# Softmax sums in four 32-column tiles, their inverses spread over partitions by DMA

## The chip, the cores and the metric

The kernel runs on one core of a Trainium2 chip. Its time is the device time of one execution in microseconds (us); before the change it is 820.48 us, the median of three runs (820.0 to 821.76). Five engines work side by side, each through its own instructions in order: TensorE (PE; its weight loads are shown as PEld), VectorE (DVE), ScalarE (ACT), GpSimd (POOL) and SyncE (SP), which here only issues DMAs. They wait for each other by semaphores.

## The reference, cut to what matters

Two transformer layers with different attention and feed-forward parts. The change lies in the attention of layer 0 alone: batch 2, sequence 1024, width 128, 16 query heads over 4 key/value groups, 64 columns a head.

```python
xn = _layernorm(x, ln_scale, ln_bias)
q = (xn @ Wq) per head; k, v = split(xn @ Wkv) per group
q, k = _layernorm(q, ...), _layernorm(k, ...)
dots = jnp.einsum('bghqd,bgkd->bghqk', qg, k) * scale
attn = jax.nn.softmax(dots, axis=-1)
out = jnp.einsum('bghqk,bgkd->bghqd', attn, v)
return out @ Wout
```

The softmax needs, for each head and query, the sum over 1024 keys of the exponentials and its inverse; the kernel multiplies by that inverse after the product with v.

## The kernel before, in words

**Slots.** The attention of a batch is done in 16 slots, one for 256 queries and one group of four heads. The four heads of a slot stand as two halves of the partitions (h = 0, 1: 64 partitions each) and two pairs side by side in the columns (hp = 0, 1: 256 columns each). So a slot's unscaled output is 128 partitions x 512 columns.

**What a slot does.** (1) Scores with queries on the partitions, in eight units (`unit_scores`, L689); VectorE takes each row's maximum (`largest`, L1276, L1278, L1280, L1290), ScalarE copies half of most units aside for it (L992). SP puts the maxima into a spare row of the queries by eight small DMAs (L416), so that (2) the scores with keys on the partitions (`tile_scores`, L709) come out with the maximum taken off. (3) ScalarE's exponentials (`exps`, L973). (4) GpSimd adds the eight tiles of exponentials up: five additions in a row (L544), and one (L549) of a pair that VectorE adds first (`add_tail`, L1298). (5) TensorE's product with v (`tile_values`, L724), in two column tiles of 64. (6) The sums over keys (`add_up`, L739): a matrix of ones of 64 columns times GpSimd's total, in two column tiles, which gives on each of a half's 64 partitions the sum of every (pair, query) column. (7) ScalarE makes a first inverse as exp(-ln(sum)) into `rinv` (`take_log` L999, `invert` L1004), VectorE improves it by one Newton step in PSUM (`correct`, L1363 and L1366). (8) ScalarE copies the output from PSUM into `ot` (`keep_out`, L980), VectorE multiplies it there by the inverse (`scale`, L1372), (9) TensorE projects it (`project_out`, L752) and VectorE adds it to x (`add`, L1381).

**Order.** It is written out by hand. `attention` of each engine runs over phases, four to a slot. With slot m's units in phases 4m to 4m+3, its exponentials' tiles run five phases behind and the product six behind; `add_up` stands at the end of phase 4m+10 on TensorE, the inverse in 4m+11 on ScalarE. VectorE corrects at the end of 4m+11 and in the middle of 4m+12 (steps 0 and 1) and scales at the end of 4m+12, behind the second maximum of that phase and ahead of those of 4m+13; in 4m+13 it adds the tail of slot m+1. TensorE projects at the end of 4m+13. Units exist up to phase 63, so scale is followed by maxima in slots 0 to 12.

TensorE may compute a new unit only when VectorE has reduced the one before (the score banks are single): `unit_scores` waits for `part_made`. SP's queue holds, for every slot in turn, the eight DMAs of its maxima, each pair behind its wait, then after both batches the loads of the two chosen experts' weights of layer 0's feed-forward part. Slot 15 of each batch is finished in the code that follows its loop. In the last phases of batch 1 VectorE also sums the rows of the first batch, chooses the experts (L1348) and makes the low parts of their weights (L1443), ScalarE the high parts (L1061); TensorE's first product with them is L1832.

Of the kernel before, what the change touches and what calls it, by code (L numbers as in the profile page):

```python
# [166 lines left out]
def up_weights(wproj):  # L167

    return wproj[:, 0:TOP * HID].rearrange("p (k f) -> p k f", f=HID)
# [7 lines left out]
def first_layer(nc, a, xv, x, ident, wt, psum, sb, sem, c):  # L177

    with ExitStack() as own:
        def mine(name, shape, dt=F32):  # L180
            return sb(name, shape, dt, own)
# [8 lines left out]
        vecs = mine("vecs", [P, 4, DH])  # L190
        cross = mine("cross", [P, 4, DH])
# [21 lines left out]
        acc = [work[:, 2 * i * UW:(2 * i + 1) * UW].rearrange("p (h q) -> p h q", h=2) for i in range(2)]  # L213
        tail = work[:, UW:2 * UW].rearrange("p (h q) -> p h q", h=2)
        ot = work[:, 3 * UW:3 * UW + WIDE]
        rinv = work[:, 3 * UW + WIDE:4 * UW]

        def spare(k):
            return space[:, (4 + k) * UW:(5 + k) * UW]

        pt = [spare(k).rearrange("p (h q) -> p h q", h=2) for k in range(TILES)]
# [8 lines left out]
        raw = wt[:, :]  # L230
        rawi = wt[:, W_GATE * P:].bitcast(I32)
        diagonal = rinv[:, 0:P]
        aside_at = [xnt[:, 0, i * 512:(i + 1) * 512] for i in range(2)]

        x_in = [sem(f"x_in{b}") for b in range(BATCH)]
# [60 lines left out]
        pool_added = sem("pool_added")  # L296
        pv_made = sem("pv_made")
        out_kept = sem("out_kept")
        sums_made = sem("sums_made")
        log_made = sem("log_made")  # L300
        rinv_made = sem("rinv_made")
        fix_made = sem("fix_made")
        ot_made = sem("ot_made")
        y_made = sem("y_made")
# [38 lines left out]
        def banks(first, n):  # L343
            return psum[:, first * 512:(first + n) * 512]
# [16 lines left out]
        sums = banks(7, 1)  # L361
        LAST = BATCH * SLOTS - 1

        def sums_of(n):

            return banks(5, 1) if n == LAST else sums

        def rows(h):
            return slice(h * DH, (h + 1) * DH)

        def place(m):
            return divmod(m, GROUPS)

# [12 lines left out]
        def queries(t, m):  # L386
            at, g = place(m)
            return t[:, PAIRS * g:PAIRS * (g + 1), at * QB:(at + 1) * QB]

        def sync_part(sp):  # L390
            for h in range(2):
                sp.dma_start(x[:, 0, h * T:(h + 1) * T], xv[0][:, h * T:(h + 1) * T]).then_inc(x_in[0], 16)
            sp.dma_start(wproj[:, K_AT:K_AT + KV], a["L0_attn_Wkv"][:, 0:KV]).then_inc(wkv_in, 16)
            sp.dma_start(wproj[:, V_AT:V_AT + KV], a["L0_attn_Wkv"][:, KV:2 * KV]).then_inc(wkv_in, 16)
            sp.dma_start(wproj[:, Q_AT:Q_AT + INNER], a["L0_attn_Wq"]).then_inc(wq_in, 16)
            sp.dma_start(x[:, 1], xv[1]).then_inc(x_in[1], 16)
            sp.dma_start(raw[:, 0:2 * P].rearrange("p (t d) -> p t d", t=2), a["L1_attn_Wu"].rearrange("(t p) d -> p t d", p=P)).then_inc(r_in, 16)
            sp.dma_start(raw[:, 2 * P:4 * P].rearrange("p (t d) -> p t d", t=2), a["L1_attn_Wv"].rearrange("(t p) d -> p t d", p=P)).then_inc(r_in, 16)
            sp.dma_start(raw[:, 4 * P:5 * P], a["L1_attn_Wb"]).then_inc(r_in, 16)
            sp.dma_start(raw[:, W_O * P:W_GATE * P], a["L1_attn_Wo"]).then_inc(r_in, 16)  # L400
            sp.dma_start(rawi[:, 0:HID1].rearrange("p (t d) -> p t d", t=HT), a["L1_ffn_w_gate"].rearrange("(t p) d -> p t d", p=P)).then_inc(r_in, 16)
            sp.dma_start(rawi[:, HID1:2 * HID1].rearrange("p (t d) -> p t d", t=HT), a["L1_ffn_w_up"].rearrange("(t p) d -> p t d", p=P)).then_inc(r_in, 16)
            sp.dma_start(rawi[:, 2 * HID1:3 * HID1], a["L1_ffn_w_down"]).then_inc(r_in, 16)
            sp.dma_start(wout[:, :, :], a["L0_attn_Wout"].rearrange("(h p) d -> p h d", p=P)).then_inc(wout_in, 16)
            for dst, src in small:
                sp.dma_start(dst, src).then_inc(shared_in, 16)
            for b in range(BATCH):
                for m in range(SLOTS):
                    n = SLOTS * b + m
                    at, g = place(m)  # L410
                    sp.wait_ge(ql_made, TILES * b + 2 * at + 2)
                    for pair in range(4):
                        t, hp = divmod(pair, PAIRS)
                        sp.wait_ge(max_made, 4 * n + pair + 1)
                        for h in range(2):
                            sp.dma_start(ql[h * DH:h * DH + 1, PAIRS * g + hp, at * QB + t * P:at * QB + (t + 1) * P].bitcast(F32),  # L416
                                         nmx[n % 2][:, pair, h:h + 1], allow_slow_non_contiguous=True).then_inc(max_placed[n % 2], 16)
            sp.wait_ge(chosen0_made, 1)
            es = [sp.value_load(chosen[0:1, 0, k:k + 1], min_val=0, max_val=EXPERTS - 1) for k in range(TOP)]
            for k, e in enumerate(es):  # L420
                sp.dma_start(up_weights(wproj)[:, k, :], a["L0_ffn_W1"][bass.ds(e, 1), :, :].rearrange("e d f -> d (e f)")).then_inc(c["up_in"][0], 16)
            for k, e in enumerate(es):
                sp.dma_start(c["b1s"][:, 0, k, :], a["L0_ffn_b1"][bass.ds(e, 1), :].rearrange("e (t f) -> f (e t)", f=P), allow_slow_non_contiguous=True).then_inc(c["b1_in"][0], 16)
            for k, e in enumerate(es):
                sp.dma_start(down_weights(wproj)[:, k, :, :], a["L0_ffn_W2"][bass.ds(e, 1), :, :].rearrange("e (t f) d -> f (e t) d", f=P)).then_inc(c["down_in"][0], 16)
                sp.dma_start(c["b2s"][:, 0, k, :], a["L0_ffn_b2"][bass.ds(e, 1), :]).then_inc(c["down_in"][0], 16)
# [130 lines left out]
        def tensor_part(pe):  # L557
# [170 lines left out]
            def add_up(n):  # L728

                if n and n < LAST:  # L730
                    pe.wait_ge(x_added, n)
                terms = [acc[n % 2]]
                if n % SLOTS == SLOTS - 1:
                    terms = [pt[TILES - 2], pt[TILES - 1], acc[n % 2]]
                for k, term in enumerate(terms):
                    if k == len(terms) - 1:
                        pe.wait_ge(pool_added, ADDS * (n + 1))
                    for h in range(2):
                        last = pe.matmul(sums_of(n)[rows(h), :], c["ones_square"][:, 0:DH], term[:, h, :],  # L739
                                         start=(k == 0), stop=(k == len(terms) - 1))  # L740
                last.then_inc(sums_made, 1)
# [145 lines left out]
        def scalar_part(act):  # L887
# [106 lines left out]
            def take_log(n):  # L994

                act.wait_ge(sums_made, n + 1)
                if n:
                    act.wait_ge(ot_made, n)
                act.activation(rinv, sums_of(n), ACT.Ln).then_inc(log_made, 1)  # L999

            def invert(n):

                act.wait_ge(log_made, n + 1)
                act.activation(rinv, rinv, ACT.Exp, scale=-1.0).then_inc(rinv_made, 1)  # L1004

            def produce(b):

# [144 lines left out]
        def vector_part(dve):  # L1152
# [198 lines left out]
            def weights_of_chosen():  # L1351
# [4 lines left out]
                route_link(dve.reciprocal(wv[:, 0, 0:1], r[:, 6, 1:2]))  # L1356
                dve.tensor_tensor(wv[:, 0, 1:2], wv[:, 0, 0:1], r[:, 6, 0:1], ALU.mult).then_inc(wv0_made, 1)

            def correct(n, step):

                if step == 0:
                    dve.wait_ge(rinv_made, n + 1)
                    dve.tensor_tensor(sums_of(n), sums_of(n), rinv, ALU.mult).then_inc(fix_made, 1)  # L1363
                else:
                    dve.wait_ge(fix_made, 2 * n + 1)
                    dve.scalar_tensor_tensor(out=sums_of(n), in0=sums_of(n), scalar=2.0, in1=rinv, op0=ALU.subtract, op1=ALU.mult).then_inc(fix_made, 1)  # L1366

            def scale(n):

                dve.wait_ge(fix_made, 2 * n + 2)  # L1370
                dve.wait_ge(out_kept, n + 1)
                dve.tensor_tensor(ot, ot, sums_of(n), ALU.mult).then_inc(ot_made, 1)  # L1372

            def add(n):

# [25 lines left out]
            def attention(b, end):  # L1401

                for ph in range(LAG + 1, end):
                    mine_at, mine_k = divmod(ph, 4)
                    m, k = divmod(ph - LAG - 5, 4)
                    n = SLOTS * b + m
                    if mine_at < SLOTS:
                        largest(SLOTS * b + mine_at, 2 * mine_k)
                    if k == 0 and 0 < m <= SLOTS:
                        add(n - 1)  # L1410
                    if k == 2 and 0 <= m < SLOTS:
                        correct(n, 1)
                    if mine_at < SLOTS:
                        largest(SLOTS * b + mine_at, 2 * mine_k + 1)
                    if k == 1 and 0 <= m < SLOTS:
                        correct(n, 0)
                    if k == 2 and 0 <= m < SLOTS:
                        scale(n)
# [953 lines left out]
```

## Time and profile before

| | |
|---|---|
| median of three runs | 820.48 us |
| profiled execution | 819.98 us, span 818.2 |
| instructions | 14237 |
| HBM traffic | 5.92 MB read, 1.05 MB written |
| DMA | 49745 packets, 8.03 MB |

The rows of the trace are given as times in microseconds from the span's start. In a timeline or a chain the first number is the start, the second the length; "x8" counts instructions that are merged into one row, and the bracket says how long the engine was idle before and who ended it. Only compute counts as busy; matmul ends are modelled.

### The profile page before, as it was taken

Reading aid. Unit: us, or ns where it says so; the run is one execution under the profiler, and the core shown is the slowest. Engines: PE = TensorE matmul, PEld = TensorE weight load, DVE = VectorE, ACT = ScalarE, POOL = GpSimd, SP = SyncE. Lnnn points to the kernel's source line nnn. Section 1 sums busy time; section 2 is a strip of 40 time slices with the busy share of each in tenths; the row PEclk is TensorE's granted clock in tenths of the full one; section 3 lists DMA queues with packets and bytes.
Section 4 is the critical chain, followed back from the end, with each engine's and each line's share of the span. In section 5 each row is a group of like instructions: output and inputs, shape, how many; then the busy total and the mean of one; then the engine's idle time right before and its main releaser. Section 6 shows DMA issues by size and latency. Waiting matters only on the chain.

```text
span 818.2 us, 14237 instructions
## 1 busy us (share of the span) xinstructions
PE 790.9 (97%) x5002; PEld 474.4 (58%) x5002; DVE 631.3 (77%) x1147; ACT 524.8 (64%) x955; POOL 589.1 (72%) x385
## 2 busy tenths in 40 slices
PE   6998999999999999999899999999999999999998
PEld 5664455455555555566544555555555555987787
DVE  6997788888888787376867788887888877678774
ACT  3865576676667776668655766666777666555522
POOL 2777587888888888946558888788988796455840
PEclk9999999999999999999999999999999999999999
DMA  6000000000000000000000000000000002200001
GB/s 183 1 2 1 0 2 2 1 1 1 1 1 2 1 2 1 1 1 1 1 1 2 1 1 1 2 1 2 1 1 1 2 1 53 56 1 2 1 1 52
DMA packets 49745, 8.03 MB, mean 10 GB/s; under 512 B 42502, under 2 KB 48266, under 8 KB 49674
## 3 DMA queue, kind: packets, MB, share of 16 engines
q1 hardware_dynamic: 48810, 6.99, 5.4%
q8 instruction: 40, 0.66, 0.4%
q14 instruction: 31, 0.25, 0.1%
q10 hardware_dynamic: 864, 0.13, 0.1%
HBM read 5.92 MB, written 1.05 MB: 9 GB/s over the span
## 4 chain that ended last, share of the span: by engine, by line
PE 88%; DVE 6%; ACT 2%; issue 2%; POOL 1%; DMA 1%; SPq 0%; DVEq 0%; POOLq 0%; ACTq 0%
PE psum L724 29%; PE psum L709 21%; PE psum L689 10%; PE psum L739 4%; PE psum L1846 4%; PE psum L752 3%; DVE part L1280 2%; PE psum L1857 2%; PE psum L575 2%; PE psum L1884 2%; PE psum L577 1%; PE psum L576 1%; PE psum L1914 1%; PE psum L1832 1%; PE psum L668 1%
## 5 line engine op out<-in xcount | busy, mean ns | idle before, releaser
L544 POOL TENSOR_TENSOR space<-space 128x1024 f32<-128x1024 f32 x160 | 381.6, 2385 | 23.7 <-ACT space L973 5.7
L973 ACT ACTIVATE space<-psum 128x512 f32<-128x512 f32 x512 | 264.2, 606 | 37.2 <-PE psum L709 36.3
L724 PE MATMUL psum<-space,vb 128*64 128x512 f32 x1024 | 247.5, 605 | 2.1 <-ACT space L973 2.1
L1280 DVE TENSOR_REDUCE part<-psum 128x2 f32<-128x1024 f32 x150 | 183.0, 1220 | 32.0 <-PE psum L689 32.0
L724 PEld LDWEIGHTS psum<-space,vb 128*64 128x64 f32 x1024 | 62.5, 136 | 120.3 <-issue 60.8
L549 POOL TENSOR_TENSOR space<-space 128x1024 f32<-128x1024 f32 x30 | 71.7, 2389 | 79.8 <-DVE space L1298 79.8
L689 PE MATMUL psum<-kh,qh 64*128 64x512 f32 x512 | 119.0, 453 | 4.5 <-DVE part L1280 4.5
L1276 DVE TENSOR_REDUCE part<-psum 128x1 f32<-128x512 f32 x106 | 73.2, 690 | 53.4 <-PE psum L689 53.4
L709 PE MATMUL psum<-qh,kh 64*128 64x512 f32 x512 | 105.8, 395 | 0.0
L709 PE MATMUL psum<-qh,kl 64*128 64x512 f32 x512 | 105.2, 389 | 0.0
L689 PEld LDWEIGHTS psum<-kh,qh 64*128 64x128 f32 x512 | 49.9, 183 | 95.4 <-DVE part L1280 57.4
L709 PE MATMUL psum<-ql,kh 64*128 64x512 f32 x512 | 104.9, 390 | 0.0
L992 ACT ACTIVATE xnt<-psum 128x512 f32<-128x512 f32 x106 | 63.1, 595 | 47.7 <-PE psum L689 47.7
L1278 DVE TENSOR_REDUCE part<-xnt 128x1 f32<-128x512 f32 x106 | 72.6, 685 | 1.9 <-ACT xnt L992 0.3
L709 PEld LDWEIGHTS psum<-qh,kl 64*128 64x128 f32 x512 | 51.9, 184 | 7.7
L709 PEld LDWEIGHTS psum<-qh,kh 64*128 64x128 f32 x512 | 50.5, 185 | 10.0 <-ACT space L973 3.2
L709 PEld LDWEIGHTS psum<-ql,kh 64*128 64x128 f32 x512 | 51.6, 184 | 8.0
L999 ACT ACTIVATE space<-psum 128x512 f32<-128x512 f32 x32 | 19.2, 600 | 52.0 <-PE psum L739 52.0
L1298 DVE TENSOR_TENSOR space<-space 128x512 f32<-128x512 f32 x60 | 46.0, 807 | 2.7 <-ACT space L973 2.7
L980 ACT ACTIVATE space<-psum 128x512 f32<-128x512 f32 x32 | 19.2, 599 | 43.0 <-PE psum L752 41.7
L1747 POOL TENSOR_TENSOR inv<-inv,half_power 128x4 f32<-128x4 f32 x18 | 18.7, 1043 | 38.0 <-DVE inv L2095 26.3
L752 PEld LDWEIGHTS psum<-wout,space 128*64 128x64 f32 x512 | 30.0, 137 | 17.8 <-issue 17.1
(252 smaller groups left out, 1134.5 us busy)
## 6 DMA issues: line engine op xcount, KB each, us to landing
ql<-nmx SPq DMA_DIRECT2D x256, 0.5 KB, 2.0
wproj<-in_L_ffn_W SPq DMA_DIRECT2D x4, 256.0 KB, 3.5
out<-x SPq DMA_DIRECT2D x3, 256.0 KB, 2.0
x<-in_L_attn_x SPq DMA_DIRECT2D x2, 256.0 KB, 4.4
wproj<-in_L_attn_Wq SPq DMA_DIRECT2D x1, 512.0 KB, 6.6
x<-in_L_attn_x SPq DMA_DIRECT2D x1, 512.0 KB, 7.5
wout<-in_L_attn_Wout SPq DMA_DIRECT2D x1, 512.0 KB, 7.1
w1s<-in_L_ffn_W SPq DMA_DIRECT2D x2, 256.0 KB, 2.8
```

Source lines behind the costliest of these rows:

```text
L544: pool.tensor_tensor(to, pt[0] if u == 1 else to, pt[u], ALU.add)\
L549: pool.tensor_tensor(to, to, tail, ALU.add).then_inc(pool_added, 1)
L689: last = pe.matmul(scores[:, h * 512:(h + 1) * 512], qh[rows(h), PAIRS * g + hp, at * QB + t * P:at * QB + (t + 1) * P], kh[rows(h), g, ha ...
L709: last = pe.matmul(key_scores[kt % 2][h].rearrange("p (a q) -> p a q", a=PAIRS), key[rows(h), g, keys], queries(query[rows(h)], m), start= ...
L724: last = pe.matmul(outp[rows(h), :], vb[:, place(m)[1], kt, :], pt[kt][:, h, :], start=(kt == 0), stop=(kt == TILES - 1))
L752: last = pe.matmul(sums_of(n)[rows(s), t * P:(t + 1) * P], ot[:, at:at + DH], wout[:, PAIRS * g + hp, :], start=(hp == 0), stop=(hp == PAI ...
L973: act.activation(pt[kt][:, h, :], key_scores[kt % 2][h], ACT.Exp).then_inc(exp_made, 1)
L992: act.activation(aside_at[i % 2], scores[:, 512:1024], ACT.Copy).then_inc(unit_kept, 1)
L1276: dve.tensor_reduce(to[:, 0, 0:1], scores[:, 0:512], AX_X, ALU.max, negate=True).then_inc(part_made, 1)
L1278: dve.tensor_reduce(to[:, 0, 1:2], aside_at[i % 2], AX_X, ALU.max, negate=True).then_inc(kept_read, 1)
L1280: dve.tensor_reduce(to[:, half, :], scores.rearrange("p (h k) -> p h k", h=2), AX_X, ALU.max, negate=True)\
L1298: dve.tensor_tensor(tail[:, h, :], pt[TILES - 2][:, h, :], pt[TILES - 1][:, h, :], ALU.add).then_inc(tail_made, 1)
```

## The change

All slots but the last of each batch (`is_brief`) form their sums in another way. The matrix of ones has 32 columns, and the four (half, pair) combinations of a slot go to four column tiles of 32 partitions, each over 256 columns. So `sums` holds 128 partitions x 256 columns, the four heads one below another. Ln, Exp and the Newton step work on that shape, in two small tiles that are free by then (`guess_at`, `brief`); both correction steps stand together in phase 4m+11. The result lies in SBUF with a head on 32 partitions, where `ot` has a head on 64 partitions of one pair's columns; so SP copies each head's 32 rows twice into `rinv` (eight DMAs of 32 x 1 KB a slot, `spread_rinv`), behind the maxima of the slot two later, and for the last of these slots ahead of what SP does next. `scale` waits for these copies and multiplies `ot` by `rinv`, both in SBUF.

```diff
+        def spread_rinv(sp, n):
+            sp.wait_ge(fix_made, 2 * n + 2)
+            for h in range(2):
+                for hp in range(PAIRS):
+                    for first in (h * DH, h * DH + DH // 2):
+                        sp.dma_start(rinv[first:first + DH // 2, hp * QB:(hp + 1) * QB], brief[brief_rows(h, hp), :]).then_inc(rinv_spread, 16)
...
                             sp.dma_start(ql[...], nmx[n % 2][:, pair, h:h + 1], ...).then_inc(max_placed[n % 2], 16)
+                    if m >= 2:
+                        spread_rinv(sp, n - 2)
+                spread_rinv(sp, SLOTS * b + SLOTS - 2)
             sp.wait_ge(chosen0_made, 1)
...
+                if is_brief(n):
+                    pe.wait_ge(pool_added, ADDS * (n + 1))
+                    for h in range(2):
+                        for hp in range(PAIRS):
+                            last = pe.matmul(sums[brief_rows(h, hp), 0:QB], c["ones_square"][:, 0:P // 4], acc[n % 2][:, h, hp * QB:(hp + 1) * QB],
+                                             start=True, stop=True)
+                    last.then_inc(sums_made, 1)
+                    return
...
+            def correct_brief(n):
+                at = sums[:, 0:QB]
+                dve.wait_ge(rinv_made, n + 1)
+                dve.tensor_tensor(at, at, guess_at, ALU.mult).then_inc(fix_made, 1)
+                dve.wait_ge(fix_made, 2 * n + 1)
+                dve.scalar_tensor_tensor(out=brief, in0=at, scalar=2.0, in1=guess_at, op0=ALU.subtract, op1=ALU.mult).then_inc(fix_made, 1)
...
             def scale(n):
-                dve.wait_ge(fix_made, 2 * n + 2)
                 dve.wait_ge(out_kept, n + 1)
-                dve.tensor_tensor(ot, ot, sums_of(n), ALU.mult).then_inc(ot_made, 1)
+                if is_brief(n):
+                    dve.wait_ge(rinv_spread, spread_count(n))
+                    dve.tensor_tensor(ot, ot, rinv, ALU.mult).then_inc(ot_made, 1)
+                else:
+                    dve.wait_ge(fix_made, 2 * n + 2)
+                    dve.tensor_tensor(ot, ot, sums_of(n), ALU.mult).then_inc(ot_made, 1)
...
-                    if k == 2 and 0 <= m < SLOTS:
+                    if k == 2 and m == SLOTS - 1:
                         correct(n, 1)
...
-                    if k == 1 and 0 <= m < SLOTS:
+                    if k == 1 and 0 <= m < SLOTS - 1:
+                        correct_brief(n)
+                    if k == 1 and m == SLOTS - 1:
                         correct(n, 0)
```

## Rows read from the trace of the kernel before

**Rows 1.** The page: busy time by engine; the chain that ended last, by engine.

```profile
PE 790.9 (97%) x5002; PEld 474.4 (58%) x5002; DVE 631.3 (77%) x1147; ACT 524.8 (64%) x955; POOL 589.1 (72%) x385
...
PE 88%; DVE 6%; ACT 2%; issue 2%; POOL 1%; DMA 1%; SPq 0%; DVEq 0%; POOLq 0%; ACTq 0%
```

**Rows 2.** Busy time in one slot: PE, PEld, DVE, ACT, POOL; clock, DMA.

```profile
193.00:210.46 17.46, 17.46 (x122) 9.33 (x120) 14.18 (x24) 12.03 (x23) 14.28 (x6) 1.00 0.04 0
```

**Rows 3.** Chain of waits in one slot: start, length (us), engine, line.

```profile
195.88 1.87 PE psum L724 x8
...
197.75 0.86 PE psum L739 x4
...
198.60 0.43 PE psum L689 x2
...
208.30 0.23 PE psum L689 x2
```

**Rows 4.** Timeline of one slot: start, us, engine, line, idle before.

```profile
202.14 0.69 DVE L1363 TENSOR_TENSOR psum<-psum,space 128x512 f32<-128x512 f32 x1
...
202.46 0.51 PE L689 MATMUL psum<-kh,qh 64*128 64x512 f32 x2
...
203.00 0.69 DVE L1276 TENSOR_REDUCE part<-psum 128x1 f32<-128x512 f32 x1 [0.17 <-PE psum L689]
...
206.29 0.69 DVE L1372 TENSOR_TENSOR space<-space,psum 128x512 f32<-128x512 f32 x1
...
206.94 0.69 DVE L1276 TENSOR_REDUCE part<-psum 128x1 f32<-128x512 f32 x1
...
208.57 1.23 DVE L1280 TENSOR_REDUCE part<-psum 128x2 f32<-128x1024 f32 x1 [0.32 <-PE psum L689]
...
210.04 1.29 DVE L1298 TENSOR_TENSOR space<-space 128x512 f32<-128x512 f32 x2
...
211.48 2.39 POOL L549 TENSOR_TENSOR space<-space 128x1024 f32<-128x1024 f32 x1 [2.61 <-DVE space L1298]
```

**Rows 5.** Groups by line: xcount, busy us, mean ns, idle before.

```profile
L1381 DVE TENSOR_TENSOR x<-x,psum 128x256 f32<-128x256 f32 x32 | 13.1, 410 | 3.1 <-PE psum L752 3.1
```

**Rows 6.** Timeline of SP's queue, in the slot and at the start.

```profile
202.25 0.47 SPq L416 DMA_DIRECT2D ql<-nmx  x1
...
202.76 0.60 SPq L416 DMA_DIRECT2D ql<-nmx  x1
...
16.86 0.91 SPq L406 DMA_DIRECT2D uvb_bias<-in_L_attn_bv  x2
```

**Rows 7.** Issues that store the output: ns min/median/max.

```profile
L1730 SPq DMA_DIRECT2D out<-x x2: 332/332/332, 814.7 to 816.0; - x2
```

**Rows 8.** DMA issues: count, KB each, median us to landing.

```profile
ql<-nmx SPq DMA_DIRECT2D x256, 0.5 KB, 2.0
...
out<-x SPq DMA_DIRECT2D x2, 128.0 KB, 1.7
```

**Rows 9.** GpSimd's timeline of the next slot.

```profile
213.84 12.49 POOL L544 TENSOR_TENSOR space<-space 128x1024 f32<-128x1024 f32 x5
```

**Rows 10.** Timelines of GpSimd and VectorE at the end of batch 0.

```profile
318.60 12.74 POOL L544 TENSOR_TENSOR space<-space 128x1024 f32<-128x1024 f32 x5
...
327.86 4.03 DVE L1298 TENSOR_TENSOR space<-space 128x512 f32<-128x512 f32 x2 [1.35 <-ACT space L973]
```

**Rows 11.** End of batch 1: VectorE's, ScalarE's timeline, then the chain.

```profile
678.28 0.15 DVE L1348 FIND_INDEX8 chosen<-router 1x8 uint32<-1x8 f32 x1
...
680.43 0.68 DVE L1363 TENSOR_TENSOR psum<-psum,space 128x512 f32<-128x512 f32 x1
...
686.11 1.99 DVE L1443 TENSOR_TENSOR up_low<-wproj,up_high 128x1024 fp32r<-128x1024 f32 x1 [3.07 <-ACT up_high L1061]
...
685.02 1.06 ACT L1061 ACTIVATE up_high<-wproj 128x1024 fp32r<-128x1024 f32 x1 [0.76 <-DMA wproj<-in_L_ffn_W]
...
690.27 0.43 PE psum L1832
```

More of the change, by code:

```diff
@@ L232, in first_layer @@
         diagonal = rinv[:, 0:P]
+        guess_at = vecs[:, :, :].rearrange("p k d -> p (k d)")
+        brief = cross[:, :, :].rearrange("p k d -> p (k d)")
         aside_at = [xnt[:, 0, i * 512:(i + 1) * 512] for i in range(2)]
@@ L301, in first_layer @@
         rinv_made = sem("rinv_made")
+        rinv_spread = sem("rinv_spread")
         fix_made = sem("fix_made")
@@ L369, in rows, with is_brief, brief_rows, spread_count @@
             return slice(h * DH, (h + 1) * DH)
+        def is_brief(n):
+            return n % SLOTS < SLOTS - 1
+        def brief_rows(h, hp):
+            first = P // 4 * (PAIRS * h + hp)
+            return slice(first, first + P // 4)
+        def spread_count(n):
+            return 16 * 8 * (n - n // SLOTS + 1)
         def place(m):
@@ L731, in add_up @@
                     pe.wait_ge(x_added, n)
-                terms = [acc[n % 2]]
-                if n % SLOTS == SLOTS - 1:
-                    terms = [pt[TILES - 2], pt[TILES - 1], acc[n % 2]]
+                if is_brief(n):
[6 more added lines that the diff above has]
+                    return
+                terms = [pt[TILES - 2], pt[TILES - 1], acc[n % 2]]
                 for k, term in enumerate(terms):
@@ L998, in take_log @@
                     act.wait_ge(ot_made, n)
-                act.activation(rinv, sums_of(n), ACT.Ln).then_inc(log_made, 1)
+                if is_brief(n):
+                    act.activation(guess_at, sums[:, 0:QB], ACT.Ln).then_inc(log_made, 1)
+                else:
+                    act.activation(rinv, sums_of(n), ACT.Ln).then_inc(log_made, 1)
             def invert(n):
                 act.wait_ge(log_made, n + 1)
-                act.activation(rinv, rinv, ACT.Exp, scale=-1.0).then_inc(rinv_made, 1)
+                at = guess_at if is_brief(n) else rinv
+                act.activation(at, at, ACT.Exp, scale=-1.0).then_inc(rinv_made, 1)
             def produce(b):
@@ L1368, in scale @@
             def scale(n):
-                dve.wait_ge(fix_made, 2 * n + 2)
                 dve.wait_ge(out_kept, n + 1)
-                dve.tensor_tensor(ot, ot, sums_of(n), ALU.mult).then_inc(ot_made, 1)
+                if is_brief(n):
+                    dve.wait_ge(rinv_spread, spread_count(n))
+                    dve.tensor_tensor(ot, ot, rinv, ALU.mult).then_inc(ot_made, 1)
+                else:
+                    dve.wait_ge(fix_made, 2 * n + 2)
+                    dve.tensor_tensor(ot, ot, sums_of(n), ALU.mult).then_inc(ot_made, 1)
             def add(n):
```

## The prediction

> **What bounds the kernel now.** I read the page first: TensorE is busy 97% of the span and carries 88% of the chain that ended last [rows 1]. An average can hide stages, so next the change's own stage: attention, 32 slots of 17.46 us. In a slot's window TensorE is busy for all of it at granted clock 1.00, VectorE 14.2 us, ScalarE 12.0, GpSimd 14.3 [rows 2]. The chain of waits inside a slot is TensorE from piece to piece; the sums that the change shrinks (L739) are 0.86 us of it [rows 3]. So a microsecond taken from TensorE in a slot is a microsecond of the kernel, as long as nothing else becomes late. The timeline then shows who has slack there: scale (L1372) starts at 206.29, and right behind it the next score maximum (L1276) at 206.94 to 207.63, which TensorE's second score unit needs when TensorE comes to it at 208.30 [rows 3, 4]. Scale can therefore start 208.30 - 207.63 = 0.67 us late before TensorE stops, and VectorE works strictly in order.

> **The change, part by part** (30 of 32 slots; the last of each batch keeps the old form).

> *TensorE, sums.* Before: 4 instructions over 512 columns, two column tiles side by side, 0.86 us [rows 3]. After: 8 over 256 columns. Four tiles truly side by side give 8 x 0.43 / 2 / 4 = 0.43 us (0.43 being one 512-column instruction of such a tile, two of which run in 0.43); if only two run at once it is 0.86 again. A change of tile shape shows as well: the two L689 instructions take 0.43 us behind L739, but 0.23 behind instructions of their own shape, so 0.20 per change [rows 3]; after the change there is one more, from 64-column to 32-column tiles. Saving per slot: 0.43 - 0.20 = 0.23 us; ends +0.43 (no price for the change of shape) and -0.20 (two at a time and the price). I take 0.23, since two 64-column tiles do run side by side.

> [...] Four column tiles at once are in no row of this kernel.

> *ScalarE and VectorE before the spread.* Ln and Exp over 256 columns instead of 512 shorten work that was not waited for: nothing. The two corrections move together into the place of L1363 at 202.14. A 128x256 operation with a PSUM operand takes 0.41 [rows 5], so with a gap of 0.03 they end at about 203.0, when L1276 starts anyway [rows 4]: nothing lost.

> *The spread.* Its eight DMAs sit on SP's queue behind the last pair of the running slot's maxima, which holds SP until 202.76 + 0.60 = 203.36 [rows 6]. SP issues one DMA at a time: 0.47 and 0.60 us in that pair (pitch 0.51 to 0.65), two of 0.43 in 0.91 at the start (pitch 0.48) [rows 6], 0.33 for an output store (pitch 0.38) [rows 7]. The first starts at 203.40. From issue to landing a small SBUF transfer takes 2.0 us, a 128 KB store 1.7 [rows 8]. So the eighth lands at 203.40 + 7 x 0.48 + 2.0 = 208.76; ends 203.40 + 7 x 0.38 + 1.7 = 207.8 and 203.40 + 7 x 0.65 + 2.0 = 209.95. I take 208.76, since 32-row transfers of 32 KB are nearest to the plain rows. Nothing covers this: scale is now an in-order wait of 208.76 - 206.29 = 2.5 us, and queued behind it on VectorE is the maximum that frees the score banks. TensorE stops for 2.5 - 0.67 = 1.8 us. On the DMA queues themselves 256 KB a slot is little; the next slot's maxima behind the spread are needed a whole phase later.

> *Scale with two SBUF operands.* Before, its factor lay in PSUM and it took 0.69. What a two-SBUF operation meets when GpSimd is adding is seen once a batch: two L1298 take 4.03 us instead of 1.29, ending about when GpSimd's five additions end (318.60 + 12.74 = 331.34; each about 2.5) [rows 10]. In a slot GpSimd runs from the end of the tail addition for 2.36 + 12.49 = 14.85 us without a break [rows 4, 9], so scale can be held by an addition that is under way.

> These two parts form a loop. From scale's start: itself 0.72, L1276 0.69, TensorE's second unit and its wake-ups 0.60 (0.51 for the pair of L689), L1280 to L1298 1.47 (208.57 to 210.04), L1298 to L549 1.44: GpSimd's chain starts 4.92 us later [rows 4] and ends 14.85 after that. If scale must wait for that end, the slot is 19.77 us: +2.31. Without the hold, by the landing alone, it is 17.46 - 0.23 + 1.84 (2.51 with the start of L1276, less 0.67) = 19.07: +1.6; by the landing's ends 18.1 to 20.3. At a slot of 19.07 the landing falls some 0.8 us before GpSimd's end, inside its last addition, so the hold decides and I take 19.77. It would decide for any landing from about 207.2 to 209.5. TensorE's 0.23 is then worth nothing: it waits anyway.

> *How often.* In slots 0 to 12 of each batch score units follow scale: 26 x 2.31 = 60 us. In slots 13 and 14 they have ended, and TensorE gains its 0.23 four times (-1), but in batch 0 scale of slot 14 comes late for the projection that follows: +1.5 by the same 5.4 us from correction to landing.

> *SP's queue at the end of batch 1.* The spread of slot 14 stands ahead of the loads of the chosen experts. Before, the choice was out at 678.43 and its weights were there for ScalarE at 685.02: 6.6 us. Now SP first waits for slot 14's correction (680.43 + 0.85 = 681.3) and issues eight DMAs (3.9): the loads start from 685.2, ScalarE at 691.8, VectorE's low part (1.1 behind it, 1.99 long) at 694.9; TensorE wanted it at 690.27 [rows 11]. That is 4.6. About 2 more (an estimate) come from scale of slot 13, late by some 2.5 us as in any slot: behind it on VectorE stand the row sums that the choice hangs on. I take +6.5 (bounds 0, if later work absorbs it, and 10).

> *Sum.* 60 - 1 + 1.5 + 6.5 = +67. The profiled execution took 819.98 us (span 818.2 and 1.8 around it), 0.5 under the median of 820.48. Forecast: 820 + 67 = 887 us.

> **Rivals.**
> 1. *The landing alone decides, GpSimd holds nothing* (scale slips between two additions, or the landing is early): 26 x 1.6 + 7 = +49, 869 us; with the early landing 26 x 0.65 + 5 = +22, 842. For it: in most slots L1298 takes its 0.69 each; against it: those run when GpSimd is idle and waits for them (2.61 us idle before L549) [rows 4].
> 2. *Late landing*, SP's pitch at 0.65: slot 20.3, 26 x 2.8 + 10 = +83, 903 us. For it: the second DMA of each pair of maxima takes 0.60. Against: those move 128 pieces of 4 bytes each.
> 3. *The spread lands in time, the kernel gets faster.* The place is scale at 206.29. It would decide if the eighth landed by 206.96, a pitch under (206.96 - 203.40 - 1.7) / 7 = 0.27 us; the least issue shown is 0.33. Then only TensorE's saving is left, 30 x 0.23 to 30 x 0.43: 807 to 813 us. [...] SP's rows of 0.33 to 0.60 speak against it.
> 4. *The tiles bring nothing and the spread is hidden*: 30 x (-0.20) the other way, 826 us, or no change.

> **How the numbers follow.** Forecast 0.55 (its own range 875 to 898), rival 1 0.24, rival 2 0.12, rival 3 0.06, rival 4 0.03. Range 845 to 904: forecast, most of rival 1, and rival 2 in its lower half; outside it rivals 3 and 4 and the extremes. A difference under 0.2% (1.6 us) can't be told from none here: faster 0.06, same 0.02, slower 0.92.

> **What would show it.** In a slot's window of the changed kernel: slot 19.8 us instead of 17.46; TensorE idle about 2.3 us ahead of the second L689 unit, released by VectorE; scale preceded by an idle stretch that a DMA ends, then longer than 0.69 itself because GpSimd runs; SP issuing eight DMAs in about 3.9 us. The sums: eight instructions in about 0.43 us with a shape change of 0.2 ahead of them. The forecast is wrong if SP's pitch is under 0.3 us, if scale never waits, or if it takes 0.69 while GpSimd adds. A lower clock in the slots would make it worse than forecast; nothing in the rows at 1.00 says that idle stretches of 2 us bring it.

## The result and the profile after

The changed kernel takes 942.93 us (median of four runs, 941.44 to 943.98) against 821.12 for the kernel before on the same chip: ratio 1.148, 95% interval 1.146 to 1.150. Forecast were 887 us and a range of 845 to 904: the sign and the place were right, the size was not. The profiled execution has a span of 941.0 us, 122.8 more than before.

The page of the changed kernel (the busy line; the chain by engine; one group: busy, mean ns | idle before it and what ended most of it):

```profile
PE 822.0 (87%) x5122; PEld 478.9 (51%) x5122; DVE 610.4 (65%) x1147; ACT 515.5 (55%) x955; POOL 586.1 (62%) x385
...
PE 54%; SPq 17%; DVE 14%; DMA 7%; issue 4%; ACT 2%; POOL 1%; DVEq 0%; POOLq 0%; ACTq 0%
...
L716 PE MATMUL psum<-kh,qh 64*128 64x512 f32 x512 | 124.1, 477 | 89.1 <-DVE part L1313 84.6
```

TensorE had 88% of the chain [rows 1]; now it has 54, and SP's issuing and DMAs have 24, where they had next to nothing. TensorE waits 84.6 us for VectorE's maximum (L1313) ahead of a score unit (L716, L689 before). What VectorE waited for stands one step further back, in the list of waits (us in total, times, longest):

```profile
DVE space L1418 <- DMA space<-cross: 130.9, 30, 7.0
PE psum L716 <- DVE part L1313: 84.6, 26, 4.5
```

Scale (L1418) waits for the spread in all 30 slots, TensorE in the 26 in which units follow, just as the forecast counted them.

A regular slot of the changed kernel, from its timeline (start, us; in brackets the idle time before and its releaser); it answers to [rows 4]:

```profile
320.43 2.40 POOL L576 TENSOR_TENSOR space<-space 128x1024 f32<-128x1024 f32 x1 [5.46 <-DVE space L1335]
...
328.70 0.42 DVE L1402 SCALAR_TENSOR_TENSOR cross<-psum,vecs 128x256 f32<-128x256 f32 x1
329.52 5.04 SPq L412 DMA_DIRECT2D space<-cross  x8
...
335.91 0.69 DVE L1418 TENSOR_TENSOR space<-space 128x512 f32<-128x512 f32 x1 [3.65 <-DMA space<-cross]
...
337.26 0.50 PE L716 MATMUL psum<-kh,qh 64*128 64x512 f32 x2 [2.86 <-DVE part L1313]
337.69 1.94 PE L751 MATMUL psum<-space,vb 128*64 128x512 f32 x8
...
340.71 2.40 POOL L576 TENSOR_TENSOR space<-space 128x1024 f32<-128x1024 f32 x1 [5.48 <-DVE space L1335]
```

From GpSimd's tail addition to the next (L576) it is 20.28 us instead of 17.46: +2.82. SP's eight issues take 5.04 us, scale starts 6.39 us after the first, and TensorE has stood still for 2.86. Scale itself takes 0.69: nothing holds it. GpSimd had ended 5.48 us ahead of 340.71, at 335.23, before scale began.

But 26 x 2.82 is only 73 of the 122.8 us. An earlier slot, of batch 0:

```profile
208.82 2.36 POOL L576 TENSOR_TENSOR space<-space 128x1024 f32<-128x1024 f32 x1 [9.55 <-DVE space L1335]
...
219.78 5.04 SPq L412 DMA_DIRECT2D space<-cross  x8
...
227.62 0.69 DVE L1418 TENSOR_TENSOR space<-space 128x512 f32<-128x512 f32 x1 [5.09 <-DMA space<-cross]
...
228.97 0.79 PE L716 MATMUL psum<-kh,qh 64*128 64x512 f32 x2 [4.30 <-DVE part L1313]
...
229.70 3.68 PE L751 MATMUL psum<-space,vb 128*64 128x512 f32 x8
...
232.72 2.36 POOL L576 TENSOR_TENSOR space<-space 128x1024 f32<-128x1024 f32 x1 [9.10 <-DVE space L1335]
```

Two things are worse here. Scale starts 7.84 us after the first issue instead of 6.39, though SP issued as fast. And when TensorE goes on after 4.30 us of standing still, its work takes almost twice as long: eight instructions of the product with v (L751) 3.68 us, where they take 1.94 in the regular slot. The windows say why (us; busy time of PE, PEld, DVE, ACT, POOL; granted clock; DMA):

```profile
229.00:231.00 2.00, 2.00 (x6) 0.79 (x8) 1.70 (x2) 0.00 (x0) 0.00 (x0) 0.50 0.00 0
...
320.43:340.71 20.28, 17.42 (x122) 8.99 (x122) 13.66 (x22) 12.88 (x28) 14.23 (x6) 1.00 0.09 14
...
380.00:383.00 3.00, 3.00 (x16) 1.50 (x14) 1.38 (x3) 0.00 (x0) 1.48 (x1) 0.50 0.05 0
```

The granted clock is 0.50 behind the longer stop; in the regular slot, with a stop of 2.86 us, it stays at 1.00. Two slots later it is 0.50 again, behind a stop of only 2.84 us that ended at 377.78. In 12 of the 26 slots with a stop the mean clock is below 1.00, 0.85 to 0.92. [rows 2] had 1.00 with no stop.

Last, the ends. The tail addition's first and last start bracket the slots of both batches (kernel before, then after):

```profile
L549 POOL TENSOR_TENSOR space<-space x30: 2347/2394/2398, 90.4 to 670.7; 128x1024 f32<-128x1024 f32 x30
```

```profile
L576 POOL TENSOR_TENSOR space<-space x30: 2345/2382/2413, 90.6 to 784.7; 128x1024 f32<-128x1024 f32 x30
```

Between them 580.3 us became 694.1 (+113.8); from the last one to the end of the span 147.5 became 156.3 (+8.8).

### The profile page after: what moved, and what is told of

It reads as the page before. It is cut to its first block, busy times and chain, and to the rows that moved or that the text cites. A ratio compares the mean times of both kernels' runs of the same rounds, so it can differ in the third digit from the quotient of the medians.

```text
span 941.0 us, 14717 instructions
## 1 busy us (share of the span) xinstructions
PE 822.0 (87%) x5122; PEld 478.9 (51%) x5122; DVE 610.4 (65%) x1147; ACT 515.5 (55%) x955; POOL 586.1 (62%) x385
## 4 chain that ended last, share of the span: by engine, by line
PE 54%; SPq 17%; DVE 14%; DMA 7%; issue 4%; ACT 2%; POOL 1%; DVEq 0%; POOLq 0%; ACTq 0%
PE psum L751 14%; SPq L412 13%; PE psum L736 10%; PE psum L716 7%; DMA space<-cross 6%; DVE part L1317 5%; PE psum L785 3%; SPq L440 3%; PE psum L1897 3%; DVE space L1418 2%; PE psum L763 2%; DVE part L1313 2%; PE psum L1908 1%; PE psum L602 1%; PE psum L1935 1%
## 5 line engine op out<-in xcount | busy, mean ns | idle before, releaser
L1006 ACT ACTIVATE space<-psum 128x512 f32<-128x512 f32 x512 | 264.0, 603 | 39.5 <-PE psum L736 37.7
L751 PE MATMUL psum<-space,vb 128*64 128x512 f32 x1024 | 268.5, 649 | 2.1 <-ACT space L1006 2.1
L716 PE MATMUL psum<-kh,qh 64*128 64x512 f32 x512 | 124.1, 477 | 89.1 <-DVE part L1313 84.6
L576 POOL TENSOR_TENSOR space<-space 128x1024 f32<-128x1024 f32 x30 | 71.3, 2377 | 196.6 <-DVE space L1335 196.6
L716 PEld LDWEIGHTS psum<-kh,qh 64*128 64x128 f32 x512 | 50.0, 188 | 180.7 <-DVE part L1313 95.7
L751 PEld LDWEIGHTS psum<-space,vb 128*64 128x64 f32 x1024 | 66.1, 144 | 128.9 <-issue 75.6
L1313 DVE TENSOR_REDUCE part<-psum 128x1 f32<-128x512 f32 x106 | 73.0, 689 | 67.2 <-PE psum L716 67.2
L1013 ACT ACTIVATE space<-psum 128x512 f32<-128x512 f32 x32 | 19.2, 599 | 163.0 <-PE psum L785 161.7
L1418 DVE TENSOR_TENSOR space<-space 128x512 f32<-128x512 f32 x30 | 21.7, 724 | 130.9 <-DMA space<-cross 130.9
L785 PEld LDWEIGHTS psum<-wout,space 128*64 128x64 f32 x512 | 35.7, 158 | 28.1 <-issue 22.3
L785 PE MATMUL psum<-wout,space 128*64 128x128 f32 x512 | 39.5, 305 | 2.3 <-DVE space L1421 1.7
```

The costliest lines, as they stand in the source:

```text
L576: pool.tensor_tensor(to, to, tail, ALU.add).then_inc(pool_added, 1)
L716: last = pe.matmul(scores[:, h * 512:(h + 1) * 512], qh[rows(h), PAIRS * g + hp, at * QB + t * P:at * QB + (t + 1) * P], kh[rows(h), g, ha ...
L751: last = pe.matmul(outp[rows(h), :], vb[:, place(m)[1], kt, :], pt[kt][:, h, :], start=(kt == 0), stop=(kt == TILES - 1))
L785: last = pe.matmul(sums_of(n)[rows(s), t * P:(t + 1) * P], ot[:, at:at + DH], wout[:, PAIRS * g + hp, :], start=(hp == 0), stop=(hp == PAI ...
L1006: act.activation(pt[kt][:, h, :], key_scores[kt % 2][h], ACT.Exp).then_inc(exp_made, 1)
L1313: dve.tensor_reduce(to[:, 0, 0:1], scores[:, 0:512], AX_X, ALU.max, negate=True).then_inc(part_made, 1)
```

## The experiments

The theory going in: the way round by SP makes scale late, that stops TensorE, and three further things make it dear: a low clock after the stops, GpSimd's hold on two-SBUF operations (or not), and SP's queue at the end of batch 1. Rivals: the four-tile sums themselves lose, the DMA traffic itself costs, or the hold is the main term.

**1. Without the spread, factor from PSUM.** The kernel leaves out the placing of the inverses, so its output is not the layer's. The edits below are shown against the changed kernel where nothing else is said; "..." marks what is left out.

```diff
-                    if m >= 2:
-                        spread_rinv(sp, n - 2)
-                spread_rinv(sp, SLOTS * b + SLOTS - 2)
...
-                    dve.wait_ge(rinv_spread, spread_count(n))
-                    dve.tensor_tensor(ot, ot, rinv, ALU.mult).then_inc(ot_made, 1)
+                    dve.wait_ge(fix_made, 2 * n + 2)
+                    halves = ot.rearrange("p (a q) -> p a q", a=PAIRS)
+                    dve.tensor_tensor(halves, halves, over_mid(sums[:, 0:QB], PAIRS), ALU.mult).then_inc(ot_made, 1)
```

> The changed kernel without the spread: no DMAs are issued, and scale multiplies by the 256 inverses in PSUM (so the product is not the softmax's; this leaves out the placing of the inverses). Theory A (all of the loss is the wait of scale for the spread, with what that wait brings on): the slot is before's 17.46 us less the saving of the 32-column tiles, 0.25 to 0.30, so 820 - 30 x 0.25 to 0.30 = 811 to 813 us, granted clock 1.00. Rival B (the tiles or the moved correction cost something themselves): 820 or more.

Measured 814.14 us, ratio 0.991 (0.988 to 0.993): theory A, 1.1 us above its range. GpSimd's tail additions in its timeline:

```profile
193.18 2.40 POOL L573 TENSOR_TENSOR space<-space 128x1024 f32<-128x1024 f32 x1 [2.33 <-DVE space L1332]
...
210.33 2.39 POOL L573 TENSOR_TENSOR space<-space 128x1024 f32<-128x1024 f32 x1 [2.33 <-DVE space L1332]
```

A slot is 17.15, 0.30 less than before. Its chain of waits shows the sums (L760) and the unit behind them, against 0.86 and 0.43 in [rows 3]:

```profile
214.06 0.57 PE psum L760 x8
214.63 0.43 PE psum L713 x2
```

Two tiles at a time would need 0.86 us for the eight instructions (an estimate: eight of 256 columns against the four of 512 in [rows 3]), so more than two of the four 32-column tiles run side by side. All of the loss is in how the inverses get to scale.

**2. The same, with a second operand in SBUF** (a weight tile in place of the inverses, which the kernel leaves out altogether). Against experiment 1:

```diff
-                    halves = ot.rearrange("p (a q) -> p a q", a=PAIRS)
-                    dve.tensor_tensor(halves, halves, over_mid(sums[:, 0:QB], PAIRS), ALU.mult).then_inc(ot_made, 1)
+                    dve.wait_ge(wout_in, 16)
+                    dve.tensor_tensor(ot, ot, wout[:, 0:4, :].rearrange("p h d -> p (h d)"), ALU.mult).then_inc(ot_made, 1)
```

> As the run before, but scale multiplies by a matrix that lies in SBUF from the start (not the inverses; their placing is left out): two SBUF operands and no wait for a DMA. Theory A (GpSimd's additions hold scale only when one is under way at its start, and that price is small): within 3 us of the run before, 811 to 816. Rival H (the hold of the prediction: scale waits for the end of GpSimd's five additions and the slot goes to 19.8 us): up to 820 + 26 x 2.3 = 880.

Measured 816.93 us (0.994, 0.992 to 0.996), 2.8 us above experiment 1: theory A. The scale line of its trace (min/median/max ns):

```profile
L1416 DVE TENSOR_TENSOR space<-space,wout x30: 693/1039/2286, 101.0 to 677.6; 128x512 f32<-128x512 f32 x30
```

The hold exists, 1039 ns at the median against 690, but at this place it is 0.35 us and within the slack of 0.67. It ranges from nothing to 1.6 us: what it costs depends on where in an addition of 2.5 us scale arrives.

**3. TensorE kept busy in its stop.**

```diff
+                    m, k = divmod(ph - LAG - 8, 4)
+                    if k == 0 and 0 <= m < SLOTS - 3:
+                        pe.wait_ge(wout_in, 16)
+                        for _ in range(6):
+                            pe.matmul(sums[:, QB:2 * QB], ident[:, :], wout[:, 0:2, :].rearrange("p h d -> p (h d)"), start=True, stop=True)
```

> The changed kernel with six matmuls of 128x256 (2.6 us, results unused) put in front of TensorE's second score unit, where it stood idle 2.85 us in most slots and 4.3 in the first six. Theory C (a part of the loss is the clock at half rate behind those idle stretches): the granted clock is back near 1.00 and the slots of 24 us go to about 21.7 (20.27 and the 1.45 by which the last landing is late there); in all some 20 us less, 920 +- 6. Rival (the slow clock hides behind waits anyway): 943 or, with the added work, a little more.

Measured 919.75 us (1.120, 1.118 to 1.122): 23 us less than the changed kernel, by adding work. One of its windows, over a slot:

```profile
203.00:223.20 20.20, 20.14 (x135) 11.14 (x134) 13.68 (x24) 11.67 (x24) 14.19 (x7) 1.00 0.09 14
```

The granted clock is 1.00 in every slot, also in those that ran partly at 0.50. Taking the low clock away was worth 23 us, net: late landings (below) fell on other slots in this run.

**4. Four DMAs instead of eight.** VectorE's second correction writes both halves of `rinv`, and SP only copies the other 32 partitions.

```diff
-                    for first in (h * DH, h * DH + DH // 2):
-                        sp.dma_start(rinv[first:first + DH // 2, hp * QB:(hp + 1) * QB], brief[brief_rows(h, hp), :]).then_inc(rinv_spread, 16)
+                    other = brief_rows(h, 1 - hp)
+                    sp.dma_start(rinv[other, hp * QB:(hp + 1) * QB], rinv[brief_rows(h, hp), hp * QB:(hp + 1) * QB]).then_inc(rinv_spread, 16)
...
-                dve.scalar_tensor_tensor(out=brief, in0=at, scalar=2.0, in1=guess_at, op0=ALU.subtract, op1=ALU.mult).then_inc(fix_made, 1)
+                dve.scalar_tensor_tensor(out=rinv.rearrange("p (a q) -> p a q", a=PAIRS), in0=over_mid(at, PAIRS), scalar=2.0,
+                                         in1=over_mid(guess_at, PAIRS), op0=ALU.subtract, op1=ALU.mult).then_inc(fix_made, 1)
```

> The changed kernel with four DMAs a slot instead of eight: VectorE writes its result to both column halves of the factor (512 columns instead of 256, +0.3 us), and only the quarters on the wrong partitions are copied. Theory A (the landing of the last of the serially issued DMAs sets the slot): it lands 4 x 0.63 - 0.3 = 2.2 us earlier, TensorE's idle stretch falls from 2.85 to about 0.6, the slot to 18.0; clock 1.00; 820 + 26 x 0.55 + 6 = 840 us. Rival H (hold by GpSimd): scale is asked for inside GpSimd's last addition and waits for its end, slot 19.8, 886 us.

Measured 878.15 us (1.071, 1.067 to 1.074), 8 us under rival H and 38 above theory A: the hold decides here. Its timeline:

```profile
224.65 2.40 POOL L576 TENSOR_TENSOR space<-space 128x1024 f32<-128x1024 f32 x1 [4.65 <-DVE space L1335]
227.00 12.45 POOL L571 TENSOR_TENSOR space<-space 128x1024 f32<-128x1024 f32 x5
...
244.11 2.41 POOL L576 TENSOR_TENSOR space<-space 128x1024 f32<-128x1024 f32 x1 [4.66 <-DVE space L1335]
```

```profile
237.57 2.43 DVE L1419 TENSOR_TENSOR space<-space 128x512 f32<-128x512 f32 x1 [1.09 <-DMA space<-space]
```

The landing falls inside GpSimd's last addition (it ends at 239.45); scale starts at 237.57 and is done only at 240.00, 0.55 after that end. The slot is 19.46, close to the 19.77 that the forecast worked out for this loop. The hold decides when the landing is early enough, and in the changed kernel it was too late for it.

TensorE's stops are about 2.0 us in this run, and they brought the low clock too: in 7 of its 26 slots with units behind scale the mean granted clock is 0.91 or 0.92 (0.979 over the whole run). These took 19.24 to 19.75 us, like the others, so here the clock cost little.

**5. Slot 14 in the old form too**, so that no spread stands ahead of the expert loads.

```diff
-            return n % SLOTS < SLOTS - 1
+            return n % SLOTS < SLOTS - 2
...
-                spread_rinv(sp, SLOTS * b + SLOTS - 2)
...
```

> The changed kernel with slot 14 of each batch in the old form too, as slot 15 is, so that no spread stands ahead of the expert loads on SP's queue at the end of batch 1. Theory A (the tails are SP's queue and slot 14's own wait): the two intervals of slot 14 fall back by about 4.3 and 1.7 us, the end of batch 1 by about 5: 943 - 11 = 932 us (928 to 936). Rival B (the late end comes from slot 13's late scale, not from the queue): 937 to 943 us.

Measured 943.25 us (1.150, 1.147 to 1.153), rival B by the total. The trace divides it:

```profile
L575 POOL TENSOR_TENSOR space<-space x30: 2345/2368/2408, 90.5 to 790.1; 128x1024 f32<-128x1024 f32 x30
```

From the last tail addition to the end (span 940.3) it is 150.2, down from 156.3: SP's queue at the end, with slot 14's own wait, was worth 6.1 us, as theory A had it there. But the slots before, in which no instruction was changed up to slot 13, took 699.6 instead of 694.1, so the gain does not show in the total. Part of it is clock; in batch 1 of this run:

```profile
642.79:665.90 23.11, 20.28 (x122) 10.19 (x120) 13.64 (x22) 11.71 (x23) 14.21 (x6) 0.88 0.08 13
```

23.11 us at a mean clock of 0.88, where TensorE had stood still for just 2.83. A stop of this length brings the low clock in some slots and not in others, and an edit elsewhere shifts which. Theory A's 4.3 and 1.7 us, between the tail additions of slots 13 and 14, did not come back: they belong to slot 13's late scale, not to slot 14's own.

**6. All eight DMAs issued, none waited for.** Scale takes the unplaced inverses from PSUM, as in experiment 1, so placing them is left out of the output here too. ScalarE and VectorE wait for the copies of the slot before they write over tiles that these use.

```diff
+                    act.wait_ge(rinv_spread, spread_count(n - 1))
                     act.activation(rinv, sums_of(n), ACT.Ln).then_inc(log_made, 1)
...
+                if n:
+                    dve.wait_ge(rinv_spread, spread_count(n - 1) if is_brief(n - 1) else spread_count(n - 2))
...
-                    dve.wait_ge(rinv_spread, spread_count(n))
-                    dve.tensor_tensor(ot, ot, rinv, ALU.mult).then_inc(ot_made, 1)
+                    dve.wait_ge(fix_made, 2 * n + 2)
+                    halves = ot.rearrange("p (a q) -> p a q", a=PAIRS)
+                    dve.tensor_tensor(halves, halves, over_mid(sums[:, 0:QB], PAIRS), ALU.mult).then_inc(ot_made, 1)
```

> All eight spread DMAs are issued as in the changed kernel, but scale takes the inverses from PSUM and does not wait for them; the spread tile is not read. Theory A (the wait is the price, the DMAs themselves are nearly free): slots of 17.2 us as without the spread, plus SP's queue at the end of batch 1 (5 to 9 us): 818 to 824 us. Rival B (SP's eight issues or the traffic delay the maxima's transfers and the other queues): slots above 18 us, 840 us or more.

Measured 819.78 us (0.998, 0.997 to 1.000), theory A. The traffic and SP's issuing cost the slots nothing:

```profile
209.11 2.39 POOL L576 TENSOR_TENSOR space<-space 128x1024 f32<-128x1024 f32 x1 [2.33 <-DVE space L1336]
...
226.27 2.39 POOL L576 TENSOR_TENSOR space<-space 128x1024 f32<-128x1024 f32 x1 [2.33 <-DVE space L1336]
```

17.16 a slot with 256 KB of spread in each. Against experiment 1 the difference in the traces lies at the end, where the expert loads stand behind the spread on SP's queue: 153.7 us from the last tail addition (662.6) to the end of the span (816.3), 148.9 there (663.9 to 812.8).

**7. and 8. Scale moved** to between the two maxima of the next phase, slot 14 in the old form; 7 with the four DMAs of experiment 4, 8 with the eight of the change.

```diff
+                    if k == 3 and 0 <= m < SLOTS and is_brief(n):
+                        scale(n)
                     if mine_at < SLOTS:
                         largest(SLOTS * b + mine_at, 2 * mine_k + 1)
-                    if k == 2 and 0 <= m < SLOTS:
+                    if k == 2 and 0 <= m < SLOTS and not is_brief(n):
                         scale(n)
...
```

> Four spread DMAs instead of eight, slot 14 in the old form, and scale moved from ahead of the two maxima of its phase to between those of the next phase, where the landing is past. Theory A (only the place of the wait costs): VectorE never waits for the landing, slots of 17.2 to 17.5 us and 812 to 822 us. Rival H (GpSimd's additions hold scale wherever it stands): a hold of up to 2.4 us, 1.7 beyond the 0.67 of slack, in each of 26 slots: 855 to 865 us.

Measured 843.74 us (1.028, 1.026 to 1.030), between both: too slow for A, less than H asked.

```profile
L1420 DVE TENSOR_TENSOR space<-space 128x512 f32<-128x512 f32 x28 | 61.4, 2193 | 8.0 <-DMA space<-space 8.0
```

The landing is hidden (8.0 us of waiting in all), but scale takes 2193 ns on average: held by GpSimd's last addition. In a regular slot:

```profile
199.33 2.36 POOL L575 TENSOR_TENSOR space<-space 128x1024 f32<-128x1024 f32 x1 [3.36 <-DVE space L1336]
201.65 12.47 POOL L570 TENSOR_TENSOR space<-space 128x1024 f32<-128x1024 f32 x5
...
217.49 2.37 POOL L575 TENSOR_TENSOR space<-space 128x1024 f32<-128x1024 f32 x1 [3.37 <-DVE space L1336]
```

```profile
212.43 2.24 DVE L1420 TENSOR_TENSOR space<-space 128x512 f32<-128x512 f32 x1
```

GpSimd ends at 214.12, scale 0.55 later, and the slot is 18.16. H's mechanism stands; its size was too large, since it took the longest hold, 2.4 us, where scale is held for 2.24 - 0.69 = 1.55.

> As the kernel with four DMAs and scale between the maxima of the next phase, but with the eight DMAs of the change. Theory A: the landing is 6.3 us after the first issue (209.7 on the clock of the kernel before), scale now stands at about 209: a wait of some 0.7 us, covered by the slack, slots of 17.2 to 17.8, 815 to 832 us. Rival H: held by GpSimd, 855 us or more.

Measured 862.02 us (1.050, 1.047 to 1.052). The total is in H's range, but scale itself took only 810 ns on average; A's wait of 0.7 came out as 1.53 in a regular slot and 66.6 us over 28 slots, 2.4 each. So neither theory has it. A regular slot is 18.18, as in 7; those with a late landing are longer, up to 20.3:

```profile
304.39 2.38 POOL L575 TENSOR_TENSOR space<-space 128x1024 f32<-128x1024 f32 x1 [3.37 <-DVE space L1336]
306.72 12.49 POOL L570 TENSOR_TENSOR space<-space 128x1024 f32<-128x1024 f32 x5
322.57 2.37 POOL L575 TENSOR_TENSOR space<-space 128x1024 f32<-128x1024 f32 x1 [3.36 <-DVE space L1336]
```

```profile
319.01 0.74 DVE L1419 TENSOR_TENSOR space<-space 128x512 f32<-128x512 f32 x1 [1.53 <-DMA space<-cross]
```

The landing and GpSimd's end (319.21) fall together here, and which of the two sets the slot stays open. Either way the two SBUF ways end 0.7 us a slot above the 17.46 of before.

**9. Spread by ScalarE within PSUM.** No DMA. The second correction writes both halves of the sums' bank, ScalarE copies four 32x256 pieces behind the exponentials of phase 4m+12, scale stands where experiments 7 and 8 put it.

```diff
+                        act.activation(sums[brief_rows(h, 1 - hp), hp * QB:(hp + 1) * QB], sums[brief_rows(h, hp), hp * QB:(hp + 1) * QB],
+                                       ACT.Copy).then_inc(rinv_spread, 1)
...
-                    dve.tensor_tensor(ot, ot, rinv, ALU.mult).then_inc(ot_made, 1)
+                    dve.tensor_tensor(ot, ot, sums[:, 0:2 * QB], ALU.mult).then_inc(ot_made, 1)
...
```

> The sums by four 32-column tiles stay; no DMA spreads the inverses. VectorE's second correction writes both halves of the sums' own PSUM bank, ScalarE copies four 32x256 pieces to the other 32 partitions behind the exps of the same phase, and scale, between the maxima of the next phase, takes its factor from PSUM. Slot 14 has the old form. Theory A (the 32-column sums are worth 0.30 us a slot, and only the way round by SP and a second SBUF operand loses): slots of 17.2 us, scale 0.69, 813 to 817 us. Rival B (four copies of about 0.35 us push the next exps or the kept unit late, and TensorE waits): slots of 17.5 to 18.2, 822 to 840 us.

Measured 817.87 us (median of five runs), ratio 0.9959 (0.9944 to 0.9974): 0.4% less than the kernel before, with the output complete. One slot of its timeline:

```profile
210.22 2.38 POOL L565 TENSOR_TENSOR space<-space 128x1024 f32<-128x1024 f32 x1 [2.40 <-DVE space L1337]
...
221.21 1.48 ACT L1023 ACTIVATE psum<-psum 32x256 f32<-32x256 f32 x4
...
223.94 0.68 DVE L1421 TENSOR_TENSOR space<-space,psum 128x512 f32<-128x512 f32 x1
...
227.44 2.38 POOL L565 TENSOR_TENSOR space<-space 128x1024 f32<-128x1024 f32 x1 [2.39 <-DVE space L1337]
```

The four copies take 1.48 us where SP's way took 6.39 from the first issue to scale, scale is 0.68 with a PSUM operand, the slot 17.22. The total is 0.9 above theory A's 817.

## Why the prediction was wrong

**The sums.** Forecast 0.23 us a slot with ends of 0.43 and -0.20; measured 0.30 (experiment 1). More than two tiles run side by side (0.57 us, where two at a time would need 0.86); if the instructions alone take the 0.43 of the forecast, the change of shape is 0.14 of the 0.57 instead of 0.20 (not measured by itself). Right, and of no use while TensorE waits.

**The landing: the step that failed.** The forecast said "So the eighth lands at 203.40 + 7 x 0.48 + 2.0 = 208.76", with the pitch taken from two starting loads. Measured is a pitch of 0.63: the chain of waits of a regular slot of the changed kernel has

```profile
393.16 0.60 SPq L412
393.75 0.04 issue
...
397.59 1.85 DMA space<-cross
```

eight issues of 0.59 to 0.60 with gaps of 0.04, then 1.85 to land. By the same formula 203.40 + 7 x 0.63 + 1.85 = 209.66, 0.9 later. The nearest rows were the pair in the slot itself, 0.47 and 0.60 [rows 6]; the forecast put the 0.60 down to its small pieces and left it to rival 2, which had the pitch at 0.65 and with it the regular slot: 20.3 forecast, 20.28 measured. That nearness is partly luck: with 209.66 the forecast's own sum gives a slot of 19.97. The rest is TensorE's own work, which the sum had at 17.46 - 0.23 = 17.23 and which is 17.42 in the regular slot (17.42 + 2.86 = 20.28); in experiment 1, without the stop, it is 17.15. Why the stop brings it back to 17.42 is open.

**The hold.** "At a slot of 19.07 the landing falls some 0.8 us before GpSimd's end, inside its last addition, so the hold decides" hung on that landing, and on the statement that it would decide for any landing from 207.2 to 209.5. 209.66 is past that, GpSimd is done, scale takes 0.69. Experiments 4 and 7 show that the hold is real where the landing is earlier (2.43 and 2.24 us for scale). So the mechanism was right and its condition not met; the slot is +2.82, not +2.31. In experiment 2 scale waits for one addition at most, and the addition behind it becomes longer too: it begins at 136.98, while scale runs until 137.38, and takes 2.65 us instead of 2.36. What in the hardware makes the two hold each other up was not shown.

**What was not priced.** The mis-sized landing explains 26 x (2.82 - 2.31) = 13 of the 56 us by which the forecast fell short. The larger part of the miss is the clock, which it put at nothing, and slots whose landing is later still, which it did not have. On top of 26 x 2.82 = 73 us the changed kernel loses:
- *The clock, 23 us net* (experiment 3); about 27 by itself (an estimate: late landings and holds add up to some 9 us in the changed kernel and 14 in experiment 3, so the net figure hides 4 to 5). The forecast saw it and put it aside: "nothing in the rows at 1.00 says that idle stretches of 2 us bring it". No row of the kernel before had TensorE idle in a slot, so rows at 1.00 could not tell; the stops of 2 us in experiment 4 did bring it (a mean of 0.91 or 0.92 in 7 slots). The trace of the kernel before has the low level once, outside the attention, behind 24 products of one column each:

```profile
776.56 2.74 PE L1871 MATMUL psum<-ones_square,prod 128*128 128x1 f32 x24
...
780.00:783.00 3.00, 3.00 (x17) 3.00 (x16) 2.75 (x14) 0.00 (x0) 0.51 (x1) 0.52 0.00 0
```

So the clock belonged into the range as a rival.
- *Late landings, about 11 us, and the hold, about 3.* With the clock at 1.00 (experiment 3) the slots still took 671.1 - 580.3 = 90.8 us more, 17.5 above 73. About 3.1 of that lies between slot 13 of a batch and the batch's end. The other 14.3 fall on the 26 slots. In 11 of them scale starts 7.0 to 7.7 us after the first issue, 11.1 us in all beyond the regular 6.38; in 8 of the 11 SP's eight issues themselves took 5.7 to 6.1 us. In two more, GpSimd's additions began 2 us late behind other work of its own, so the landing met the last one and scale took 1.75 and 1.83 us: the hold, 2.7 us in all. In the changed kernel the landing is late in the first six slots of batch 0, where scale starts 7.2 to 8.1 us after the first issue. The DMA page of the window 219.7 to 227.8 us, where scale came 7.84 us after the first issue, has

```profile
q1 hardware_dynamic: 960, 0.26, 16.9%
q8 instruction: 1, 0.02, 1.0%
```

and that of 329.4 to 336.0, with 6.39, only

```profile
q1 hardware_dynamic: 808, 0.26, 19.3%
```

In every slot of the two traces (of the changed kernel and of experiment 3) in which scale came over 7.0 us after the first issue there is a load of instructions (q8) within the spread, and none in the regular ones. That they go together is shown; that the load is the cause is not, since no kernel here was without it.
- *The ends.* Forecast -1, +1.5 and +6.5, together 7. Measured +8.8 behind the last tail addition and +3.1 before the ends of the batches (experiment 3), together 12. SP's queue, 4.6 in the forecast, is between 4.8 (experiment 6 over 1) and 6.1 (experiment 5, which also takes away slot 14's own wait).

Sum: 73.3 + 23 + 14.3 + 3.1 + 8.8 = 122.5, against 122.8 in the spans.

**What held.** That the way round loses, where TensorE stops and for whom, the 26 slots, the tails' place, and that the DMA traffic itself costs the slots nothing (17.16 us in experiment 6, 17.15 in experiment 1).

## What to carry to other kernels

Price a chain of small DMAs by issues times the slowest repeated issue of the same queue, not by the fastest (0.60 us was measured here, where the forecast took two starting loads of 0.43), and compare the landing with the place of the first instruction that waits in order behind it. When a change makes a full TensorE stop once a slot, put a rival at the lower clock (a mean of 0.85 to 0.92 in 12 of 26 slots here) into the range, since rows without stops say nothing on it. In this kernel a factor that has to reach other partitions is better moved by an engine with idle time and kept in PSUM (1.48 us on ScalarE) than sent round by eight DMAs (6.39 us) into SBUF, where GpSimd's additions held its reader (2.43 us instead of 0.69 in experiment 4).
